# Three stages of a fused decoder: other places in the queues for soft-plus, loads and parts

## What is computed

```
x = layernorm(x + delta_rule_attention(x))            # stage delta
x = layernorm(x + selective_scan(ctx, gate=x))        # stage scan
x = layernorm(x + sign_ffn(x))                        # stage sign
x = layernorm(x + landmark_attention(x))              # stage landmark
x = layernorm(x + cross_attention(x, ctx, positions)) # stage cross
x = layernorm(x + ternary_ffn(x))                     # stage ternary
```

## Time and profile before

| | |
|---|---|
| median of 3 runs | 3027.39 us (3025.77 to 3038.11) |
| the profiled execution, its own time | 3033.01 us |
| its span, first to last instruction | 3031.2 us |
| granted TensorE clock, mean over the span | 0.925 of full |
| busy over the span | PE 86%, DVE 63%, ACT 48%, POOL 38% |
| stages, us from the span's start | delta 0 to 684, scan 684 to 1206, sign to 1475, landmark to 2200, cross to 2850, ternary to the end |

### The profile page before, as it was taken

One profiled execution on the slowest core, in us unless ns is written; L12 is line 12 of the kernel. 1 busy time (PEld: TensorE's weight loads), 2 busy tenths in 40 slices (PEclk: granted clock), 3 DMA queues, 4 the chain that ended last, 5 costly groups with the idle time before them and its releaser, 6 DMA issues.

```text
span 3031.2 us, 50557 instructions
## 1 busy us (share of the span) xinstructions
PE 2622.0 (86%) x20138; PEld 1425.8 (47%) x20154; DVE 1899.5 (63%) x2978; ACT 1466.8 (48%) x2612; POOL 1153.8 (38%) x1072
## 2 busy tenths in 40 slices
PE   7899999887787866899989898888779999999787
PEld 5666666542232322788545454444433343333244
DVE  4343434438999999566266656657546666676477
ACT  4352535226666653244253543626226666666355
POOL 0555455517777766000244435162233333331000
PEclk9898999997898978999989899899879999999889
DMA  3313131412313230333243313344074445451301
GB/s 95 92 57 99 57 99 57 103 57 90 132 35 112 71 112 14 153 109 146 89 122 115 106 67 105 99 124 163 15 158 107 106 106 121 105 108 48 127 29 42
DMA packets 196766, 284.50 MB, mean 94 GB/s; under 512 B 84388, under 2 KB 86468, under 8 KB 195636
## 3 DMA queue, kind: packets, MB, share of 16 engines
q1 hardware_dynamic: 196532, 281.27, 31.8%
HBM read 192.08 MB, written 63.31 MB: 84 GB/s over the span
## 4 chain that ended last, share of the span: by engine, by line
PE 43%; DVE 10%; issue 4%; ACT 3%; DMA 2%; POOL 2%; SPq 1%; DVEq 0%; ACTq 0%; POOLq 0%
PE ps L236 8%; PE ps L3645 4%; PE ps L3658 4%; PE ps L2085 4%; PE ps L2096 4%; PE ps L3577 3%; PE ps L3594 2%; PE ps L3628 2%; PE ps L2751 1%; PE ps L2759 1%; PE ps L3582 1%; DVE arena L3014 1%; DVE arena L3012 1%; PE ps L2809 1%; ACT cross L3738 1%
## 5 line engine op out<-in xcount | busy, mean ns | idle before, releaser
L236 PE MATMUL ps<-arena 128*128 128x512 f32 (+3 forms) x1248 | 453.6, 515 | 14.9 <-ACT arena L2851 6.1
L3830 DVE TENSOR_REDUCE cross<-ps 128x1 f32<-128x512 f32 x512 | 327.8, 686 | 175.3 <-PE ps L3628 175.2
L1721 POOL TENSOR_TENSOR arena<-arena 128x1024 f32<-128x1024 f32 x128 | 305.9, 2394 | 120.8 <-DVE arena L1713 120.6
L3738 ACT ACTIVATE cross<-ps 128x512 f32<-128x512 f32 x512 | 276.7, 593 | 154.4 <-PE ps L3645 154.2
L1737 PE MATMUL ps<-arena 128*128 128x512 f32 x512 | 267.8, 665 | 39.1 <-POOL arena L1721 39.1
L1713 DVE TENSOR_TENSOR_SCAN arena<-ps,arena 128x1024 f32<-128x1024 f32 x128 | 291.6, 2279 | 9.2 <-ACT ps L1704 9.1
L236 PEld LDWEIGHTS ps<-arena 128*128 128x128 f32 (+2 forms) x1264 | 184.8, 152 | 235.4 <-issue 163.5
L1704 ACT ACTIVATE ps<-arena 128x511 f32<-128x511 f32 x256 | 164.9, 679 | 156.5 <-DVE arena L1713 156.2
L609 POOL TENSOR_TENSOR arena<-arena 128x31 f32<-128x31 f32 (+15 forms) x217 | 135.4, 624 | 200.4 <-DMA arena<-d_a 183.9
L1737 PEld LDWEIGHTS ps<-arena 128*128 128x128 f32 x512 | 105.5, 215 | 192.9 <-issue 124.8
L3645 PE MATMUL ps<-cross,cross 50*128 50x512 f32 x512 | 156.4, 506 | 31.7 <-ACT cross L3738 22.8
(11 more groups left out here) (364 smaller groups left out, 5167.8 us busy)
## 6 DMA issues: line engine op xcount, KB each, us to landing
arena<-d_bc SPq DMA_DIRECT2D x32, 1024.0 KB, 5.5
cross<-d_parts SPq DMA_DIRECT2D x192, 128.0 KB, 4.6
arena<-d_x SPq DMA_DIRECT2D x16, 1024.0 KB, 5.4
d_parts<-cross SPq DMA_DIRECT2D x32, 512.0 KB, 3.6
d_x<-arena SPq DMA_DIRECT2D x48, 256.0 KB, 2.5
arena<-in_D_wlm SPq DMA_DIRECT2D x12, 1024.0 KB, 6.3
d_signs<-arena SPq DMA_DIRECT2D x32, 256.0 KB, 2.1
arena<-arena SPq DMA_DIRECT2D x64, 128.0 KB, 2.1
```

Source lines behind the costliest of these rows:

```text
L236: ins = pe.e.matmul(ps[:m, :n], lhsT(k), rhs(k), start=(k == 0), stop=(k == chunks - 1))
L1721: pool.e.tensor_tensor(h, h, s.bc[turn % s.SLOTS][:, 1], ALU.mult).then_inc(*pool.up("scan_hC"))
L3738: act.e.activation(s.E[:, k % 2, j], s.rexp.bank((u, i)), ACT.Exp).then_inc(*s.rexp.empty(act, (u, i)))
L3830: dve.e.tensor_reduce(s.mx[:, u % 2, t, h:h + 1], s.rmax.bank((u, m)), AX.X, ALU.max, negate=True).then_inc(*s.rmax.empty(dve, (u, m)))
```

## The change

In the scan stage the input projection of chunk 0 goes from step 4 to step 7, and parts of the soft-plus of chunks 2 and 3 to later steps. In the landmark stage x of batch 1 is loaded three local steps later, and the products of paired values of batch 0 are made one local step later. In the cross stage the DMA queue has another order before its loop: the unfolds of unit 0 before the swaps of unit 1, each row maxima transfer of unit 0 earlier, the output weights behind all unfolds of the units ahead.

```diff
--- before.py
+++ after.py
@@ -1304,12 +1304,12 @@
     EARLY_ROWS = 3
     DTU, Y, FRONT, TAIL = 4, 5, 6, 7
     POOL_CONV, PE_CONV = (0,), (1, 2, 3)
-    PE_IN = {4: (0, None), 8: (1, 0), 9: (1, 1), 10: (2, 0), 11: (2, 1), 12: (3, 0), 13: (3, 1)}
+    PE_IN = {7: (0, None), 8: (1, 0), 9: (1, 1), 10: (2, 0), 11: (2, 1), 12: (3, 0), 13: (3, 1)}
     ACT_UP = {9: 0, 12: 1, 14: 2, 16: 3}
     ACT_U = {17: (0, 1), 19: (2, 3)}
     FIRST_SOFT = {"raw": {}, "abs": {0: [1]}, "ln": {2: [1]}, "floor": {1: [1]}, "log": {3: [1]}, "dt": {4: [1]}}
-    OWN_SOFT = {"raw": {0: [2], 2: [3]}, "abs": {2: [2], 4: [3]}, "ln": {8: [2, 3]}, "floor": {3: [2], 5: [3]},
-                "log": {9: [2], 10: [3]}, "dt": {10: [2], 11: [3]}}
+    OWN_SOFT = {"raw": {0: [2], 4: [3]}, "abs": {2: [2], 6: [3]}, "ln": {9: [2, 3]}, "floor": {3: [2], 7: [3]},
+                "log": {10: [2], 11: [3]}, "dt": {11: [2], 12: [3]}}
     NEXT_SOFT = {"raw": {21: [0], 23: [1]}, "abs": {24: [0], 26: [1]}, "ln": {27: [0], 29: [1]}, "floor": {25: [0], 27: [1]},
                  "log": {28: [0], 30: [1]}, "dt": {28: [0], 30: [1]}}
 
@@ -2481,7 +2481,7 @@
                     s.sp_x(sp, b + 1)
             if phase == "local" and k == T and b == B - 1:
                 s.sp_next(sp, s.dead, [sp.on("landmark_rot", B * len(s.TURNED) - 1)])
-            if phase == "local" and k == -2 and b == 0:
+            if phase == "local" and k == 1 and b == 0:
                 sp.e.wait_ge(*s.ring.at_filled(sp, ("xT", 0, T - 1)))
                 s.sp_x(sp, 1)
             if phase == "local" and k == 8:
@@ -2560,9 +2560,9 @@
             for fb, r in turned:
                 s.pool_rope(pool, fb, r)
             turned = [(fb, r) for what, fb, r in front if what == "r"]
-            if phase == "local" and b == 0 and -1 <= k < T - 1:
+            if phase == "local" and b == 0 and 0 <= k < T:
                 for i in range(2):
-                    s.pool_pairs(pool, 0, 2 * (k + 1) + i)
+                    s.pool_pairs(pool, 0, 2 * k + i)
             if phase == "global" and s.NG - 3 <= k <= s.NG and b + 1 < B:
                 for i in range(2):
                     s.pool_pairs(pool, b + 1, 2 * (k - s.NG + 3) + i)
@@ -3454,23 +3454,26 @@
         s.sp_swap(sp, 0, 0)
         s.sp_keep(sp, 0, 1)
         s.sp_keep(sp, 0, 0)
+        for w in (1, 0):
+            s.sp_unfold(sp, 0, w)
         for w in range(2):
             s.sp_swap(sp, 1, w)
-        for w in (1, 0):
-            s.sp_unfold(sp, 0, w)
-        s.sp_late(sp)
         for f in range(1, s.AHEAD):
             for w in range(2):
                 if f + 1 < s.AHEAD:
                     s.sp_swap(sp, f + 1, w)
-                s.sp_stack(sp, f, w)
-                if f + 1 == s.AHEAD and w == 0:
+                s.sp_keep(sp, f, w)
+                if (f, w) == (1, 1):
                     s.sp_rows(sp, 0, 0)
+                if (f, w) == (s.AHEAD - 1, 1):
+                    s.sp_rows(sp, 0, 1)
+                s.sp_unfold(sp, f, w)
+        s.sp_late(sp)
         for i in range(s.UNITS + 1):
             f, nb = i + s.AHEAD, i // C + 1
             if i % C == 0 and nb < B:
                 s.sp_x(sp, nb)
-            if s.unit(i) is not None:
+            if i and s.unit(i) is not None:
                 s.sp_rows(sp, i, 1)
             if i % C == 0 and i >= 2 * C:
                 s.sp_store(sp, i // C - 2)
```

## The result

The changed kernel took 3005.11 us, the median of 6 runs (3000.24 to 3016.05), against 3033.04 us for 6 runs of the kernel before beside it: ratio 0.9926, 95% interval 0.9901 to 0.9951, some 22 us. This ratio is not the quotient of the two medians, which lie 27.9 us apart. In a second timing the ratio was 0.9922 (0.9899 to 0.9944). The forecast was 18.3 us less and 3009, so the gain was larger than forecast by 4 us (by the ratio) to 10 us (by the medians). The profiled execution of after took 3000.24 us, its span 2998.5.

A forecast was written before the change was run, and what follows sets the result against it. Bound by VectorE in scan, by transfers in landmark and at the start of cross. Terms 9 + 0 + 9.3 = 18.3 us, from the median 3027.4 to 3009; likeliest case 3004 to 3013, bounds 3004.4 (2 more allowed) and 3019.

The forecast's parts named there:

- a forecast of 5: Scan, first batch: earlier decay for scan 6 and an earlier row of TensorE-paced steps gain 5 us, from 3.5 to 7.2.
- I take none: Scan: the moved logarithms meeting GpSimd's products were counted at no cost, though at most 8.7 us was possible.
- at most these 18.6 us: Scan: VectorE's remaining idle time, 18.6 us, was taken as the most the stage can give.
- The forecast of 0: Landmark, first batch: the gain of moving x is spent by the new order of the products, 0 us.
- booked at -2.9: Landmark: lower bound, -2.9 us, if x were not what delayed turn 5 and the products still came later.
- +2.8 if turn 6 were hidden: Landmark: upper bound, x's 2.8 us kept in full if turn 6 did not delay the products.
- my 55.4 for that bound: Cross start: upper bound set by TensorE's own end, at 2255.5, a gain of 10.8 + 0.3 us.
- a sign I had named for being wrong: Cross: a wait for swap 3 or the rows of unit 1 would show the forecast wrong.
- 1 (scan gives 3): Scan stage gives only 3 us while cross gives its 9.3, total 3015; chance 0.14.
- 2 (cross gives 4, the keeps land late): Cross start gives only 4 us, as two keeps each land 2.5 us later than counted, total 3014; chance 0.11.
- 3 (turn 5 not sped up): Landmark: turn 5 isn't sped up and the products' new place costs 2.9 us, total 3012; chance 0.08.
- 4 (low clock in steps 5 to 7, input of chunk 0 late): Scan, batches 1 and 2: low TensorE clock delays chunk 0's input; 9 us a batch eats all gain; chance 0.03.

## Why the forecast was right, and where it was not

**Scan.** The waits behave as forecast. In the first batch the stall before scan 6 is gone (3.48) and the row of steps under TensorE's pace ends 5.3 us earlier, 3.9 to 4.2 against the two old profiles of 524 us, for a forecast of 5. In batches 1 to 3 the idle time before scan 6 is gone too, while TensorE's projection waits just where I had placed it. The term that failed, batch by batch, is "I take none" for the logarithms. They and other short operations meet GpSimd's products, and it is not small: the waits of 1.2 to 2.0 us removed in batch 1 come out as 1.1 us (130.3 to 129.2), in batch 2 as 1.2 or even as a loss of 1.7 (127.5 and 127.6 in two old profiles, 129.2 now), and batch 3 gains 6.0 instead of some 1.6, a third of 4.7. The sum is 11.1 where I had 9; that it came so near is in part the luck of errors that cancel. In the sum over the stage their move cost nothing in the new order: with them at their old steps (one profile) the stage is 514.8 us as well, and by batches 5.9, 2.3, 1.7 and 1.6 us below the mean of the old order. So the 2 us beyond my 9 need no logarithms. In the old order the same move was worth 3 to 7 us by itself: what these meetings cost does not add up part by part. And my bound, "at most these 18.6 us", was none: it counted idle time alone, over a stretch that ends 9 us before the stage does, while 3.1 of the 13.7 us between the first two profiles came out of busy time.

**Landmark.** The forecast of 0 was wrong by the size of one of its terms: x's move gave the 2.8 us, and the products' new place, booked at -2.9, costs nothing that can be told. The failed step is that "TensorE's values(0) needs both products, and behind it stand the pooled values and the whole landmark chain". The delay of values(0) is real, 69.4 with both edits and 66.4 with x alone, but it doesn't reach the end of that chain. But in these steps GpSimd's queue sets the pace, with 7.4 us of work to a local step in the earlier trace rows (two products 2.5, the scale 1.0, a turn 3.9) and no gaps between them. It does the same operations in either order, so when it starts 2.8 us sooner it ends the row 2.8 us sooner; what moves between its neighbours only shifts where TensorE waits. The bound that I gave as "+2.8 if turn 6 were hidden" was the value. The further 1 us up to the 16th scale, and 1.2 of the mean behind it, are not explained; the latter lies within what executions of one order differ by.

**Cross.** 9.5 for 9.3 up to the first exponentials, and by the mechanism: the row maxima, sent early, were what the loop had waited for. The keeps went as counted: the unfold of k of unit 1 was issued 50.7 us after the stage's first matmul, the landing of its keep had been put at 50.4. The loop's first matmul then did not wait for that unfold, as I had it, but started when TensorE came to the end of its maxima, 58.1 us: my 55.4 for that bound was too early by the 1.6 us of the first maxima (33.7 for 32.1) and 1 us of their length. The unfold landed at 58.2 to 59.7 us where its landing is recorded, for 57.2 in my sum, and held up the maxima of unit 1 by 0.4 to 1.4 us in four profiles. So the end of the maxima and this landing came within some 2 us of each other, and by the first values (72.4 us in the mean before, 63.6 now) the start of cross gains 8.8 us. The output weights, which I counted in the way of the keeps, were not. Behind it swap 3 was late as foreseen, and cost TensorE 0.5 to 2.8 us at the rows of unit 1: that is a sign I had named for being wrong, and I had put it at nothing. What the order of cross is worth in the time of the launch stays open between 2 us lost and 10 gained.

**Rivals.** 1 (scan gives 3): no, 11. 2 (cross gives 4, the keeps land late): not by its mechanism, since in the five profiles of the new order the unfold of k was issued 0.3 to 1.2 us after my time, not the 5 that it needs; its 4 us for the whole launch are not excluded. 3 (turn 5 not sped up): no, turn 5 came 3.0 sooner. 4 (low clock in steps 5 to 7, input of chunk 0 late): the scan stage has granted clock 0.89 after and, from its first scan to its end, 0.88 before, and batches 1 and 2 are not longer than in the profile of before (batch 2 is, by 1.7 us, against the two shorter old profiles).

## What to carry to other kernels

Where one engine's queue runs without gaps through several steps, cost a reordering by when that queue starts and ends, not by the first of its results that comes later. Before pricing an edit, look for the one short transfer that stands behind others in a queue although its data are long there; here two transfers of 8 KB sent 13 us earlier were worth 8 us, while 1024 KB moved out of the way were worth nothing, because they had landed before the next transfer that matters was due. Look also at what a marker depends on: the first exponentials could not show a late keep, the next matmul could. And take more than one profile before explaining a difference of a few us: in this kernel two profiled executions of one program differ by 9.9.

## What the runs showed of the hardware

A VectorE operation on 4 numbers a partition took 0.16 or 2.34 us in the same batch of two kernels, by whether it started 0.01 us ahead of a GpSimd product or 0.02 behind; in batches 1 and 2 of the changed kernel, behind a GpSimd sum of 1.09 us (L1668), it took 1.07. A whole batch of the scan stage changes by up to 4.4 us with the step in which some logarithms stand, and one order of all engines came out as 127.5 and 130.4 us in the same batch in different executions. In most of the kernels with the new tables, on the other hand, the batches repeat to 0.1 us.
